# A selective scan by items of one state and 1024 tokens in place of two states and 512 tokens

## The reference, cut to what matters

```python
left, right = jnp.split(y @ W_up + b_up, 2, axis=-1)
left = jax.nn.silu(_causal_dwconv(left, conv_w, conv_b))
# u = left, 128 channels; 64 states
delta = jax.nn.softplus(u @ W_delta + b_delta)
Bm = u @ W_B
Cm = u @ W_C
def step(h, inputs):
    u_t, d_t, b_t, c_t = inputs
    dA = jnp.exp(d_t[..., None] * A)
    h = dA * h + (d_t * u_t)[..., None] * b_t[:, None, :]
    y = jnp.einsum('bdn,bn->bd', h, c_t)
    return (h, y)
# left = ys + u * D
gated = left * jax.nn.silu(right)
return x + gated @ W_down + b_down
```

## Time and profile before

| | us |
|---|---|
| median of three runs | 4562.25 |
| lowest, highest | 4562.19, 4566.79 |
| the profiled execution | 4572.77 |
| its span | 4571.0 |
| TensorE busy in the span | 4084.4 (89%) |
| VectorE | 3323.2 (73%) |
| ScalarE | 2541.6 (56%) |
| GpSimd | 2382.1 (52%) |

### The profile page before, as it was taken

The page is one execution under the profiler, slowest core; times in us unless marked ns, Lnnn a source line. Parts: engine busy times, 40 slices in busy tenths (PEclk is TensorE's granted clock), DMA queues, the critical chain, the costliest instruction groups (busy, mean ns, idle before and its releaser), DMA issues. The chain is left out here.

```text
span 4571.0 us, 63922 instructions
## 1 busy us (share of the span) xinstructions
PE 4084.4 (89%) x22996; PEld 3215.1 (70%) x22996; DVE 3323.2 (73%) x4687; ACT 2541.6 (56%) x4869; POOL 2382.1 (52%) x1652
## 2 busy tenths in 40 slices
PE   8899999979999999789999866689998999899975
PEld 7799999967899999656666545556666666566653
DVE  5466666655666666438788889888788787878777
ACT  6644444446444444367766643366666766666654
POOL 3100000032000000147667639789899998989887
PEclk9999999989999999899999858899999999999986
DMA  2010000010000000125444322455555565556568
GB/s 86 22 33 24 20 24 23 24 48 32 29 24 20 24 23 24 55 98 159 142 153 153 117 78 71 116 164 152 166 174 164 158 172 157 166 154 171 159 185 311
DMA packets 242095, 465.67 MB, mean 102 GB/s; under 512 B 33905, under 2 KB 154482, under 8 KB 241778
## 3 DMA queue, kind: packets, MB, share of 16 engines
q1 hardware_dynamic: 217202, 428.01, 29.2%
q0 software_dynamic: 24576, 33.57, 4.0%
HBM read 392.16 MB, written 69.34 MB: 101 GB/s over the span
## 5 line engine op out<-in xcount | busy, mean ns | idle before, releaser
L1560 POOL TENSOR_TENSOR scan_drive_sb<-scan_b_wide_sb,scan_du_sb 128x1024 f32<-128x1024 f32 x512 | 1304.7, 2567 | 241.4 <-DVE scan_h_sb L1472 234.7
L1472 DVE TENSOR_TENSOR_SCAN scan_h_sb<-decay_bank,scan_state_sb,scan_drive_sb 128x512 f32<-128x512 f32 x896 | 1107.7, 1267 | 135.8 <-ACT decay_bank L1810 125.8
L1810 ACT ACTIVATE decay_bank<-scan_delta_sb,a_neg_sb 128x512 f32<-128x512 f32 x1024 | 699.0, 686 | 263.8 <-DVE scan_h_sb L1472 261.0
L1479 DVE TENSOR_TENSOR scan_ch_sb<-c_pair,scan_h_sb 128x1024 f32<-128x1024 f32 x512 | 616.3, 1204 | 155.3 <-PE c_pair L1647 152.6
L1658 PEld LDWEIGHTS y_bank<-identity_sb,scan_ch_sb 128*128 128x128 f32 x4096 | 542.3, 151 | 191.1 <-issue 107.1
L1658 PE MATMUL y_bank<-identity_sb,scan_ch_sb 128*128 128x128 f32 x4096 | 641.3, 288 | 3.8 <-ACT scan_temp_sb L1828 3.8
L977 PE MATMUL ybank<-v_low_hi_lo_sb,pt_hi_b_sb 128*128 128x384 f32 x2048 | 622.1, 340 | 9.6 <-DVE pt_lo_b_sb L859 9.6
L912 POOL TENSOR_TENSOR acc_b_sb<-acc_b_sb,g_in_b_sb 128x256 f32<-128x256 f32 x64 | 47.2, 738 | 1101.2 <-DVE acc_b_sb L895 1101.2
L1647 PE MATMUL c_pair<-scan_cc_sb,select_state_sb 128*128 128x512 f32 x1024 | 445.1, 518 | 186.2 <-DVE scan_ch_sb L1479 185.3
L1014 ACT ACTIVATE p_b_sb<-scores,softmax_cols_b_sb 128x1024 f32<-128x1024 f32 x256 | 285.7, 1116 | 533.1 <-DVE softmax_cols_b_sb L853 395.9
L978 PE MATMUL ybank<-v_low_hi_lo_sb,pt_lo_b_sb 128*128 128x256 f32 x2048 | 574.2, 280 | 0.0
(11 more groups left out here) (302 smaller groups left out, 8112.7 us busy)
## 6 DMA issues: line engine op xcount, KB each, us to landing
scan_b_wide_sb<-b_scratch SPq DMA_DIRECT2D x512, 512.0 KB
x_b_sb<-x SPq DMA_DIRECT2D x16, 512.0 KB, 4.1
x_res_b_sb<-x SPq DMA_DIRECT2D x64, 128.0 KB, 2.3
g_in_b_sb<-g_scratch SPq DMA_DIRECT2D x64, 128.0 KB, 2.2
x_scratch<-x_res_b_sb SPq DMA_DIRECT2D x64, 128.0 KB, 1.7
xn_scratch<-xn_out_b_sb SPq DMA_DIRECT2D x64, 128.0 KB, 1.7
scan_xn_sb<-xn_scratch SPq DMA_DIRECT2D x16, 512.0 KB
moe_x_sb<-xn_scratch SPq DMA_DIRECT2D x16, 512.0 KB, 5.6
```

What stands on the lines that cost most here:

```text
L1472: e.tensor_tensor_scan(k.h[i % H_BUFFERS][:, j, :], k.decay_banks[S % DECAY_BANKS][:, :], k.drive[i % DRIVE_BUFFERS][:, j, :], start, ALU. ...
L1479: e.tensor_tensor(k.ch[i % CH_BUFFERS][:, :, :], k.c_bank[:, :, :], k.h[i % H_BUFFERS][:, :, :], ALU.mult).then_inc(k.s_ch, 1)
L1560: e.tensor_tensor(k.drive[i % DRIVE_BUFFERS][:, :, :], k.b_wide[i % B_BUFFERS][:, :, :], k.du[c % 2][:, :].unsqueeze(1).broadcast_to([P, P ...
L1810: e.activation(k.decay_banks[S % DECAY_BANKS][:, :], k.delta[c % 2][:, :], ACT.Exp, scale=wt.a[:, n:n + 1]).then_inc(k.s_decay, 1)
```

## The change

The scan's item becomes one state over 1024 tokens (two chunks, `WIDE`): 8 wides of 64 states, again 512 items. `broadcast_b` on TensorE puts B into one of two PSUM tiles of 128 x 1024; `drive` is on VectorE and multiplies it in place by delta*u; `recur` is one scan of 128 x 1024, with the decay from SBUF (a ring of three, one Exp each) and the drive from PSUM. C goes out to memory and comes back by a broadcast load, and `read_out` (C*h) is on GpSimd. `y_bank` has two banks; PSUM holds y 2, drive 4, fills 2. Preparation and `down` use plain fp32 matmuls, one where there were three, and the splits are gone, also for the weights. Two chunks are prepared before the first item, and `down` covers two chunks in 17 steps. In the combine, groups 14 and 15 wait until the scan is over.

By the order of steps item 0 now comes at step 116, the choice begins at item 110, the chosen experts at item 154, the combine at item 473; groups 8 to 13 of the combine stand at items 501 to 503, groups 14 and 15 behind the scan's last step.

```diff
@@ -1043,27 +1043,24 @@
 CHUNK = 512
 CHUNKS = SEQ // CHUNK
 ALL_CHUNKS = BATCH * CHUNKS
+HALVES = 2
+WIDE = HALVES * CHUNK
+WIDES = ALL_CHUNKS // HALVES
+WIDES_OF = CHUNKS // HALVES
 INNER = 128
 STATES = 64
-PAIR = 2
-LAG = 2
-AHEAD = 2
-PAIRS = STATES // PAIR
-ITEMS = ALL_CHUNKS * PAIRS
+ITEMS = WIDES * STATES
...
-DECAY_BANKS = 3
+DECAY_BUFFERS = 3
+DRIVE_BANKS = 2
 H_BUFFERS = 3
 CH_BUFFERS = 2
-B_BUFFERS = 3
-DRIVE_BUFFERS = 3
-B_AHEAD = 4
+C_BUFFERS = 3
+C_AHEAD = 2
 
 
...
-def scan_order(prepare, load_residual, load_b, broadcast_c, drive, recur, decay, read_out, add_up, keep, down):
-
-    yield from prepare(0)
+def halves(prepare, W):
+    for half in range(HALVES):
+        yield from prepare(HALVES * W + half)
+
+
+def down_steps(step, W):
+
+    for s in range(DOWN_STEPS):
+        for half in range(HALVES):
+            if 0 <= s - HALF_LAG * half < HALF_STEPS:
+                step(HALVES * W + half, s - HALF_LAG * half)
+        yield
+
+
+def scan_order(prepare, load_residual, load_c, broadcast_b, decay, drive, recur, read_out, keep, add_up, y_out, down):
+
+    yield from halves(prepare, 0)
     helpers = Helpers()
-    for i in range(-B_AHEAD, ITEMS + LAG + 1):
-        if i + B_AHEAD < ITEMS:
-            c, m = divmod(i + B_AHEAD, PAIRS)
-            if m == PAIRS // 2:
-                load_residual(c)
-            if m == 0 and c > 0:
+    for i in range(-C_AHEAD, ITEMS + LAG):
+        if i + C_AHEAD < ITEMS:
+            W, m = divmod(i + C_AHEAD, STATES)
+            if m == STATES // 2:
+                for half in range(HALVES):
+                    load_residual(HALVES * W + half)
+            if m == 0 and W > 0:
                 helpers.end_down()
                 helpers.end_ahead()
-            if m == LAG + B_AHEAD + 1 and c + 1 < ALL_CHUNKS:
-                helpers.ahead = prepare(c + 1)
-            load_b(i + B_AHEAD)
-        if 0 <= i - 1 < ITEMS:
-            broadcast_c(i - 1)
-        if 0 <= i + AHEAD < ITEMS:
-            drive(i + AHEAD)
-        for j in range(PAIR):
-            S = PAIR * i + j
-            if 0 <= S + 2 < PAIR * ITEMS:
-                decay(S + 2)
-            if 0 <= S < PAIR * ITEMS:
-                recur(S)
-            if 0 <= S - PAIR * LAG < PAIR * ITEMS:
-                add_up(S - PAIR * LAG)
-            if j == 0:
-                helpers.step()
-                yield
+            if m == LAG + C_AHEAD + 1 and W + 1 < WIDES:
+                helpers.ahead = halves(prepare, W + 1)
+            load_c(i + C_AHEAD)
+        if 0 <= i + 1 < ITEMS:
+            broadcast_b(i + 1)
+            decay(i + 1)
+        if 0 <= i < ITEMS:
+            drive(i)
+        helpers.step()
+        yield
+        if 0 <= i < ITEMS:
+            recur(i)
         if 0 <= i - 1 < ITEMS:
             read_out(i - 1)
             keep(i - 1)
-        if 0 <= i - LAG < ITEMS:
-            c, m = divmod(i - LAG, PAIRS)
-            if m == PAIRS - 1:
-                helpers.down.insert(0, down(c))
+        if 0 <= i - LAG + 1 < ITEMS:
+            add_up(i - LAG + 1)
+            W, m = divmod(i - LAG + 1, STATES)
+            if m == STATES - 1:
+                for half in range(HALVES):
+                    y_out(HALVES * W + half)
+                helpers.down.append(down_steps(down, W))
         helpers.step()
         yield
...
+    def load_c(i):
+        W, n = divmod(i, STATES)
+        w.wait_ge(k.s_c_saved, 16 * HALVES * (W + 1))
+        w.wait_ge(k.s_ch, i - C_BUFFERS + 1)
+        e.dma_start(k.c_wide[i % C_BUFFERS][:, :], c_dram[W][n, :].partition_broadcast(P)).then_inc(k.s_c[i % C_BUFFERS], 16)
...
-    def recur(S):
-        i, j = divmod(S, PAIR)
-        c, n = divmod(S, STATES)
-        w.wait_ge(k.s_decay, S + 1)
+    def drive(i):
+        W, n = divmod(i, STATES)
+        bank = k.drive_banks[i % DRIVE_BANKS][:, :]
+        w.wait_ge(k.s_b, i + 1)
+        w.wait_ge(k.s_du, HALVES * (W + 1))
+        e.tensor_tensor(bank, bank, k.du[W % 2][:, :], ALU.mult).then_inc(k.s_drive, 1)
+
+    def recur(i):
+        W, n = divmod(i, STATES)
+        w.wait_ge(k.s_decay, i + 1)
         w.wait_ge(k.s_drive, i + 1)
         w.wait_ge(k.s_kept, i - H_BUFFERS + 1)
         w.wait_ge(k.s_ch, i - H_BUFFERS + 1)
-        start = 0.0 if c % CHUNKS == 0 else k.state[:, n:n + 1]
-        e.tensor_tensor_scan(k.h[i % H_BUFFERS][:, j, :], k.decay_banks[S % DECAY_BANKS][:, :], k.drive[i % DRIVE_BUFFERS][:, j, :], start,
+        start = 0.0 if W % WIDES_OF == 0 else k.state[:, n:n + 1]
+        e.tensor_tensor_scan(k.h[i % H_BUFFERS][:, :], k.decay[i % DECAY_BUFFERS][:, :], k.drive_banks[i % DRIVE_BANKS][:, :], start,
                              ALU.mult, ALU.add).then_inc(k.s_scan, 1)
-
-    def read_out(i):
-        w.wait_ge(k.s_c, i + 1)
-        w.wait_ge(k.s_scan, 2 * (i + 1))
-        w.wait_ge(k.s_y, PAIR * (i - CH_BUFFERS + 1))
-        e.tensor_tensor(k.ch[i % CH_BUFFERS][:, :, :], k.c_bank[:, :, :], k.h[i % H_BUFFERS][:, :, :], ALU.mult).then_inc(k.s_ch, 1)
 
...
-    def drive(i):
-        c = i // PAIRS
-        w.wait_ge(k.s_b[i % B_BUFFERS], 16 * (i // B_BUFFERS + 1))
-        w.wait_ge(k.s_du, c + 1)
-        w.wait_ge(k.s_scan, PAIR * (i - DRIVE_BUFFERS + 1))
-        e.tensor_tensor(k.drive[i % DRIVE_BUFFERS][:, :, :], k.b_wide[i % B_BUFFERS][:, :, :],
-                        k.du[c % 2][:, :].unsqueeze(1).broadcast_to([P, PAIR, CHUNK]), ALU.mult).then_inc(k.s_drive, 1)
+    def read_out(i):
+        w.wait_ge(k.s_c[i % C_BUFFERS], 16 * (i // C_BUFFERS + 1))
+        w.wait_ge(k.s_scan, i + 1)
+        w.wait_ge(k.s_y, i - CH_BUFFERS + 1)
+        e.tensor_tensor(k.ch[i % CH_BUFFERS][:, :], k.c_wide[i % C_BUFFERS][:, :], k.h[i % H_BUFFERS][:, :], ALU.mult).then_inc(k.s_ch, 1)
...
-            e.matmul(bank, wt.up_hi[:, ci, cols], k.yt_hi[:, ci, :], start=(ci == 0), stop=False)
-            e.matmul(bank, wt.up_hi[:, ci, cols], k.yt_lo[:, ci, :], start=False, stop=False)
-            last = e.matmul(bank, wt.up_lo[:, ci, cols], k.yt_hi[:, ci, :], start=False, stop=(ci == DC - 1))
+            last = e.matmul(bank, wt.up[:, ci, cols], k.yt[:, ci, :], start=(ci == 0), stop=(ci == DC - 1))
...
-    def from_u(c, hi, lo, *key):
-        w.wait_ge(k.s_u_lo, c + 1)
-        bank = fills.take(w, *key)[0:hi.shape[1], :]
-        e.matmul(bank, hi, k.u_hi[:, :], start=True, stop=False)
-        e.matmul(bank, hi, k.u_lo[:, :], start=False, stop=False)
-        e.matmul(bank, lo, k.u_hi[:, :], start=False, stop=True).then_inc(fills.filled(*key), 1)
-
-    def b_and_c(c, m):
-        cols = slice(0, STATES if m == 0 else P)
-        from_u(c, wt.bc_hi[:, m, cols], wt.bc_lo[:, m, cols], "bc", c, m)
+    def from_u(c, weights, what):
+        fills.wait_emptied(w, "conv", c)
+        bank = fills.take(w, what, c)[0:weights.shape[1], :]
+        e.matmul(bank, weights, k.u[c % len(k.u)][:, :], start=True, stop=True).then_inc(fills.filled(what, c), 1)
...
-    def broadcast_c(i):
-        c, m = divmod(i, PAIRS)
-        fills.wait_emptied(w, "bc", c, 1)
-        w.wait_ge(k.s_ch, i)
-        for j in range(PAIR):
-            n = m * PAIR + j
-            last = e.matmul(k.c_bank[:, j, :], wt.select[:, n:n + 1].broadcast_to([P, P]), k.cc[c % 2][:, :], start=True, stop=True)
-        last.then_inc(k.s_c, 1)
-
-    def add_up(S):
-        i, j = divmod(S, PAIR)
-        c, n = divmod(S, STATES)
+    def broadcast_b(i):
+        W, n = divmod(i, STATES)
+        for half in range(HALVES):
+            fills.wait_emptied(w, "b", HALVES * W + half)
+        w.wait_ge(k.s_scan, i - DRIVE_BANKS + 1)
+        for half in range(HALVES):
+            cols = slice(half * CHUNK, (half + 1) * CHUNK)
+            last = e.matmul(k.drive_banks[i % DRIVE_BANKS][:, cols], wt.select[:, n:n + 1].broadcast_to([P, P]), k.bb[W % 2][:, cols],
+                            start=True, stop=True)
+        last.then_inc(k.s_b, 1)
+
+    def add_up(i):
+        W, n = divmod(i, STATES)
         w.wait_ge(k.s_ch, i + 1)
         if n == 0:
-            w.wait_ge(k.s_y_out, c)
-        for t in range(GT):
+            w.wait_ge(k.s_y_out, HALVES * W)
+        for t in range(HALVES * GT):
             tokens = slice(t * P, (t + 1) * P)
-            last = e.matmul(k.y_bank[:, tokens], k.ch[i % CH_BUFFERS][:, j, tokens], consts.identity[:, :], start=(n == 0 and t == 0),
+            last = e.matmul(k.y_bank[:, tokens], k.ch[i % CH_BUFFERS][:, tokens], consts.identity[:, :], start=(n == 0 and t % GT == 0),
                             stop=(n == STATES - 1), is_transpose=True, skip_group_check=True)
         last.then_inc(k.s_y, 1)
...
-    def decay(S):
-        c, n = divmod(S, STATES)
-        w.wait_ge(k.s_delta, c + 1)
-        w.wait_ge(k.s_scan, S - DECAY_BANKS + 1)
-        e.activation(k.decay_banks[S % DECAY_BANKS][:, :], k.delta[c % 2][:, :], ACT.Exp, scale=wt.a[:, n:n + 1]).then_inc(k.s_decay, 1)
+    def decay(i):
+        W, n = divmod(i, STATES)
```

(12 more changed lines are left out.)

424 lines of the change are left out of this document (180 added, 244 removed).

## The result

| | before | after |
|---|---|---|
| median, us (11 runs each) | 4562.25 | 4578.37 |
| lowest, highest | 4555.29, 4566.79 | 4572.01, 4584.11 |
| the profiled execution, its span | 4572.77, 4571.0 | 4578.37, 4576.6 |

The ratio after / before is 1.0034, 95% interval 1.0024 to 1.0043: **slower by 16 us, 0.34%**. 4520 was forecast, 4465 to 4620 was the range. The time lies in the range, on the wrong side of 4562.

The account below looks back on a forecast made before the run. It took GpSimd as the fullest engine, beside a C-bank loop between VectorE and TensorE. Terms 55 - 86 + 13 - 72 + 68 - 20 = -42 took the median 4562 to 4520 us; range 4465 to 4620.

Parts of the forecast that it names:

- Prices of instructions: VectorE per item: product in place in PSUM 1.20 us, scan of 1024 some 2.3, sum 3.5, nothing gained or lost.
- Start +55: Stretch up to the first scan: 32 more steps (46 us) and the second chunk's own matmuls (some 9), range 46 to 64.
- shared -86: Shared experts' stage: 110.5 items at 4.50 us, 497 against 583, with the wait on C gone.
- combine +68: Combine stage: 39 items left where 23 were, 159 us against 91, range 50 to 85.
- Preparation in plain fp32: Plain matmuls in preparation and down: 1.1 us more per chunk, 18 over 16 chunks, counted as 0.035 per item.
- Chosen experts, -72: Chosen experts' stage: GpSimd as floor, 318.5 items at 4.47 us for 4.69, 1424 against 1496.
- Loads ... cost nothing: SP's load queue: as long as before, loads issued two items (over 8 us) ahead, so no cost.
- The waits of 107.1 and 94.1 should shrink most here: Chosen experts: VectorE's wait for TensorE's bank and TensorE's for C·h shrink, the bank having 3.5 us to fill, not 2.44.
- rival B: The wait moves: scan, GpSimd's C·h and transposes follow one another, pace stays 4.63 and 4.69; +42, 4604 us; chance 0.24.
- Floors by averages: Chosen experts: GpSimd's busy 1361.32 over 320 items gives floor 4.25 us, less 0.1, plus gaps, 4.34 or so.
- Choice, +13: Choice stage: VectorE's round step meets GpSimd's C·h and nears the whole 2.36 us; 0.9 more for 15 items.
- End, -20: From last scan to end: 17 us to the last residual, 10 for two groups and store; 27 against 47, range -28 to -8.

Follow-up runs that it names:

- e1: Kernel before with only plain fp32 preparation and down, one matmul for three, no splits: 4521.24 us, ratio 0.9911.
- e8: Changed kernel with the next chunk's xn load issued in the previous chunk and the residual's loads 16 items later: 4567.11 us, ratio 1.0005.
- e2: Changed kernel with the sum one item later (LAG 4) and three C·h buffers for two: 4563.44 us, ratio 0.9994.
- e3: Changed kernel with the drive's product on VectorE left out but for one column: 4559.62 us (one run).
- e4: Changed kernel with C·h on GpSimd over 512 of the 1024 tokens, that half fed to all transposes: 4435.45 us (one run).
- e5: e1 with GpSimd's drive computed for one of the item's two states and used by both scans: 4460.55 us (one run).
- e9: e1 with C·h on VectorE left out but for one column of each state: 4460.14 us (one run).
- e11: Changed kernel with the edits of e2 and e8 together: 4538.91 us, ratio 0.9952.

## Why the prediction was wrong, point by point

- **Prices of instructions: right.** Product in place 1.21 for 1.20, scan 2.29 to 2.35 for 2.3, VectorE's cadence 3.51 to 3.56 for 3.5.
- **Start +55, shared -86, combine +68: right** (+51, -88, +75). The steps counted from the program's order carried these, and the shared stage took 4.48 per item for 4.50. The reason given for that pace was half right: VectorE's wait for a bank of TensorE did not go there but fell from 44.2 to 34.0 us, and the granted clock was 0.99 for 0.97.
- **Preparation in plain fp32.** "I count 0.035 per item, inside the 10% that TensorE idles" was right in that the exchange paid. In the changed kernel's stage of the chosen experts the new plain matmuls start 0.86 apart per 512 columns (L1575, L1588, middle value), as the row had it. TensorE's busy time in layer 1, over the six windows, is 2276.5 in before, 2265.6 in e1 and 2277.1 in after, but the granted clock of these profiles is 0.941, 0.948 and 0.946, and by an estimate, busy time in inverse proportion to the clock, this alone takes 17 off in e1 and 12 in after: the sums neither show the 18 nor refute them. The prediction put 0.19 per item, 60 us, on the splits that go; e1 measured 46.5 in that stage. By the Trainium skill's four passes ("FP8 and Floating Point Precision", TensorE Precision Notes) the prediction's estimate was 1.03 per 512 columns and 37 us; the 0.86 is below it.
- **Chosen experts, -72: the step that failed.** It measured -1.8. Of the forecast, 60 came from the splits and 12 from the new items; e1 shows the first (46.5), while the new items cost +44.7. The choice, which missed by 34 the other way, hides half of this in the sum. Two sentences were wrong. "**Loads ... cost nothing**": the cover I named was that a load is issued two items ahead. That holds for C, but SP's queue is one for all loads, and the xn load stands behind a C load that waits for GpSimd's newest work; before, the B load waited for a drive that ran ahead. e8 gives back 15 of the stage. "**The waits of 107.1 and 94.1 should shrink most here**": they became 119.9 and 94.4. The bank is free earlier, but the broadcast stands in TensorE's queue behind the experts' matmuls and behind the transposes of a C·h that GpSimd delivers late. e2, which takes the lateness out of that queue, gives back 16, both together 46.6, all of the loss; the wait for the bank stays at 91.4 to 98.8 even then, near e1's 105.4 for C. This is rival B, with 4.69 per item as written there, in this stage only; in the shared stage the pace was the forecast's.
- **Floors by averages.** I divided GpSimd's busy time by the items (4.25) and took what lies above it as what a change of waits can win. e3, e4, e5 and e9 show that the busy share says little here: with the items of before the fullest engine gave back 20 of 343, and the same engine 95 of 342 with the new ones.
- **Choice, +13: wrong sign**, -20.9, of which 11.4 come with the fp32 part. I had the round's step late against C·h; it comes 0.05 us earlier and takes 0.16, which makes 12 us less over the rounds where I had 13 more; e1, with the old items, still has 19.0. The rule quoted from the Trainium skill ("SBUF — State Buffer", Who interferes with whom), that the later of the two waits, agrees with VectorE's time in both rows; I had the wrong one as the later. That GpSimd waits in its turn, 0.11 us here, can't be read from its 2.37 against 2.34 undisturbed.
- **End, -20: half of it**, -10.4. "from C·h (2.35) to the last residual I estimate 17, two thirds of the 28": it is 26.9. The splits and the waits on them went, but there are two chunks' eight tiles, for which the 17 had no term of their own, and half of each tile's 2.3 is a bias product of one row, as before. The last two groups and the store took 9.6, for the 10 forecast.
- **What would show it**: the wait for the B bank was to be under 60 and is 119.9; GpSimd was to be over 95% busy with the chosen experts and is 89%; L2277 was to be near 2.3 once per item and is 0.16; from the last scan to the end it was to be under 32 and is 36.5. Of the marks set for B, the item is over 4.6 with 4.69, and TensorE's wait for C·h, 94.4, is just short of the 100.

**The best versions.** e1 at 4521 is the fastest kernel that does all of the work, 41 us under before: before's items with the fp32 part of the change. e11, the whole change mended, is at 4539.

**Still open**: whether the two mendings give more together than apart; which of the splits' costs and waits e1's 41 us are; and whether a start with one chunk, which the 1024-token items don't allow as written, would bring e11 to e1.

## What to carry to other kernels

Before moving work to an engine with room, ask whether it runs ahead there or stands between two steps of the chain: take half of its work away in a trial kernel and read the stage, since here the busy share did not tell. List every instruction that stands behind a changed wait in each queue, the loads' queue first. And when a change is made of two edits, price and time them apart: here one gave 41 us and the other took 57.

## What the runs showed of the hardware

- VectorE multiplies a 128 x 1024 PSUM tile in place in 1.21 us, the same as a product from PSUM into SBUF (1.20).
- A plain fp32 matmul whose stationary operand has a single row costs as much as one with 128 rows: its two records take 1.22 us together for 256 columns at 1.2 GHz, and so do the two of `down` beside it.
- One plain fp32 matmul takes 0.86 us per 512 columns from start to start (L1575 and L1588 of after, at a granted clock of 0.97), and the three fp32r ones that it replaces take 0.74 to 0.78 (before, 0.96).
- A one-element product of VectorE with two SBUF operands takes 0.16 us when it starts 0.05 us before a product of GpSimd with two SBUF operands, and 1.30 when it starts inside one, until that one's end.
